# Three-round graph network on one core: the first layer's matrix applied to the features before the sum over adj

## What is computed

```python
# out = relu(adj @ x @ kernel + bias)
x = _layernorm(x + gcn(x, adj))
u = x
for _ in range(3):
    v = mlp(adj @ u, uv_W1, uv_b1, uv_W2, uv_b2, uv_W3, uv_b3)
    u = mlp(adj @ v, vu_W1, vu_b1, vu_W2, vu_b2, vu_W3, vu_b3)
return _layernorm(x + v)
```

## Time and profile before

| | |
|---|---|
| median of 3 runs | 1174.88 us (1174.84 to 1175.34) |
| the profiled execution, its time | 1174.89 us |
| its span, first to last instruction | 1173.1 us, mean granted TensorE clock 0.999 |
| TensorE, matmuls | busy 1153.4 us (98%), 5220 records |
| VectorE | busy 738.6 us (63%) |
| ScalarE | busy 665.0 us (57%) |
| DMA | 260.7 MB on the main queue, 63.8% of 16 engines |

### The profile page before, as it was taken

One profiled execution on the slowest core, in us unless ns is written; L12 is line 12 of the kernel. 1 busy time (PEld: TensorE's weight loads), 2 busy tenths in 40 slices (PEclk: granted clock), 3 DMA queues, 4 the chain that ended last, 5 costly groups with the idle time before them and its releaser, 6 DMA issues.

```text
span 1173.1 us, 13671 instructions
## 1 busy us (share of the span) xinstructions
PE 1153.4 (98%) x5220; PEld 950.3 (81%) x5220; DVE 738.6 (63%) x885; ACT 665.0 (57%) x815; POOL 0.2 (0%) x4
## 2 busy tenths in 40 slices
PE   7999999999999999999999999999999999999997
PEld 6778888888888888888888888888888888887775
DVE  7997776358555555655545746554566555668885
ACT  7765554346554555555444754554556454567885
POOL 0000000000000000000000000000000000000000
PEclk9999999999999999999999999999999999999999
DMA  9998775567366646555656736655665565569891
GB/s 367 408 365 273 242 282 199 180 215 285 110 215 215 195 164 208 205 194 184 205 188 216 256 105 226 208 169 186 203 227 185 192 205 208 196 233 354 291 325 37
DMA packets 73361, 261.61 MB, mean 223 GB/s; under 512 B 8144, under 2 KB 8784, under 8 KB 73296
## 3 DMA queue, kind: packets, MB, share of 16 engines
q1 hardware_dynamic: 73296, 260.74, 63.8%
HBM read 258.61 MB, written 2.10 MB: 222 GB/s over the span
## 4 chain that ended last, share of the span: by engine, by line
PE 90%; DMA 5%; DVE 3%; ACT 2%; issue 0%; SPq 0%; ACTq 0%
PE agg_ps L790 27%; PE agg_ps L783 27%; PE agg_ps L776 27%; DMA adj_raw<-in_adj 5%; PE pre_ps L719 4%; DVE adj_lo L673 2%; PE hid_ps L681 1%; PE hid_ps L683 1%; PE hid_ps L682 1%; ACT adj_hi L561 1%; PE hid_ps L731 1%; ACT resid L483 0%; DVE stats L571 0%; PE hid_ps L745 0%; DVE resid L586 0%
## 5 line engine op out<-in xcount | busy, mean ns | idle before, releaser
L673 DVE TENSOR_TENSOR adj_lo<-adj_raw,adj_hi 128x1024 fp32r<-128x1024 f32 x488 | 578.1, 1221 | 240.6 <-ACT adj_hi L561 233.6
L776 PE MATMUL agg_ps<-adj_hi,feat_hi 128*128 128x512 f32 x1536 | 608.9, 396 | 8.1 <-ACT adj_hi L561 8.1
L783 PE MATMUL agg_ps<-adj_hi,feat_lo 128*128 128x512 f32 x1536 | 599.1, 390 | 0.0
L561 ACT ACTIVATE adj_hi<-adj_raw 128x1024 fp32r<-128x1024 f32 x488 | 494.1, 1052 | 93.3 <-PE agg_ps L790 76.9
L790 PE MATMUL agg_ps<-adj_lo,feat_hi 128*128 128x512 f32 x1536 | 474.8, 390 | 1.8 <-DVE adj_lo L673 1.8
L776 PEld LDWEIGHTS agg_ps<-adj_hi,feat_hi 128*128 128x128 f32 x1536 | 288.9, 188 | 70.3 <-issue 11.7
L790 PEld LDWEIGHTS agg_ps<-adj_lo,feat_hi 128*128 128x128 f32 x1536 | 288.0, 188 | 64.4 <-DVE adj_lo L673 4.3
L783 PEld LDWEIGHTS agg_ps<-adj_hi,feat_lo 128*128 128x128 f32 x1536 | 289.0, 188 | 62.2 <-issue 3.4
L462 ACT ACTIVATE hid<-hid_ps,params 128x512 f32<-128x512 f32 (+1 forms) x80 | 54.5, 681 | 55.5 <-PE hid_ps L683 50.3
L527 ACT ACTIVATE in_hi<-part 128x512 fp32r<-128x512 f32 x24 | 15.2, 634 | 110.7 <-DVE part L662 110.7
L462 ACT ACTIVATE post<-pre 128x512 f32<-128x512 f32 x39 | 24.6, 630 | 79.6 <-DVE pre L642 79.6
(11 more groups left out here) (56 smaller groups left out, 262.4 us busy)
## 6 DMA issues: line engine op xcount, KB each, us to landing
adj_raw<-in_adj SPq DMA_DIRECT2D x488, 512.0 KB, 5.7
resid<-in_x SPq DMA_DIRECT2D x8, 256.0 KB, 8.8
out<-resid SPq DMA_DIRECT2D x7, 256.0 KB, 6.6
params<-in_weights SPq DMA_DIRECT2D x1, 386.0 KB, 8.1
out<-resid SPq DMA_DIRECT2D x2, 128.0 KB, 1.7
b_row<-in_bias_rows SPq DMA_DIRECT2D x1, 128.0 KB, 8.7
params<-in_weights SPq DMA_DIRECT2D x1, 64.0 KB, 7.2
b_row<-in_bias_rows SPq DMA_DIRECT2D x1, 64.0 KB, 8.8
```

Source lines behind the costliest of these rows:

```text
L561: act.activation(adj_hi[:, plan.slot[b], i * CHUNK:(i + pieces) * CHUNK], adj_raw[:, h % RAW, 0:pieces * CHUNK], ACT.Copy).then_inc(adj_hi ...
L673: dve.tensor_tensor(adj_lo[:, plan.slot[b], slot], adj_raw[:, h % RAW, 0:pieces * CHUNK], adj_hi[:, plan.slot[b], slot].bitcast(F32), ALU. ...
L776: pe.matmul(group_bank(g), feat_hi[feats][:, tile(src, i)], adj_hi[:, plan.slot[b], piece(i)], start=start, stop=False)
L783: pe.matmul(group_bank(g), feat_lo[feats][:, tile(src, i)], adj_hi[:, plan.slot[b], piece(i)], start=False, stop=False)
```

## The change

For hidden units the third layer is made like the second (`product` with hid2_hi and hid2_lo, new tiles, into pre_ps), so nodes lie on the columns, and the bias is a column that the activation of `act_post` adds. Then `pe_fold`, new, multiplies post by the first matrix of the next pass's network (four fp32 matmuls of 128 columns, which turn the tile), into the same bank pre_ps; `act_feat` copies it, rounded, to feat_hi and `dve_feat` subtracts. So the features of passes 2 to 5 are already multiplied by W1, and there `act_in`, `dve_in` and `pe_hid1` are gone: `act_hid1` works on the sum itself. Pass 1, whose features come from the layernorm, keeps the first layer (kinds IN_1 and TURN_1). The last pass loses it as well. `dve_pre` is left for the gcn and the last pass. The weights to split are five and no longer four. The table of steps is new (the kind TURN before and now, and TURN_1, are shown), the spill of a begun part to SBUF stands no earlier than act_hid1 of the unit that reads the same place, and TensorE's pe_out waits for the feat_lo of the unit before.

```diff
-    TURN: dict(dve_sum=0, act_in=0, dve_in=0, pe_hid1=4, act_hid1=5, dve_hid=4, pe_hid2=9, act_hid2=11,
-               pe_out=12, dve_pre=12, act_post=15, dve_feat=17),
...
+    TURN_1: dict(dve_sum=1, act_in=2, dve_in=2, pe_hid1=5, act_hid1=6, dve_hid=5, pe_hid2=8, act_hid2=9,
+                 dve_hid2=10, pe_out=13, act_post=14, pe_fold=16, act_feat=17, dve_feat=18),
...
+    TURN: dict(dve_sum=0, act_hid1=1, dve_hid=0, pe_hid2=4, act_hid2=5, dve_hid2=6, pe_out=9, act_post=10,
+               pe_fold=12, act_feat=13, dve_feat=14),
...
-            after_last = {"dve_pre": ends.get("dve_stats", -1), "act_std": ends.get("dve_shift", -1),
+            after_last = {"act_hid1": ends.get("pe_hid2", -1), "pe_out": ends.get("dve_feat", -1), "dve_pre": ends.get("dve_stats", -1), "act_std": ends.get("dve_shift", -1),
                           "dve_stats": ends.get("dve_norm", -1),
                           "act_post": max(ends.get("act_norm", -1) if self.steps_of(u) != END else -1,
-                                          ends.get("act_post", -1))} if tiles[0] == 0 else {}
+                                          ends.get("act_post", -1), ends.get("pe_fold", -1))} if tiles[0] == 0 else {}
...
-        return TURN if r in (0, self.rows - 1) else IN_PARTS
+        turn = r in (0, self.rows - 1)
+        if s == 1:
+            return TURN_1 if turn or r < 3 else IN_1
+        return TURN if turn else IN_PARTS
...
-    HID_W = {UV: (0, 1), VU: (2, 3), LAST: (0, 1)}
-    OUT_W = {GCN: 0, UV: 5, VU: 6, LAST: 5}
-    OUT_BIAS = {GCN: 0, UV: 1, VU: 2, LAST: 1}
+    N_WEIGHTS, N_SPLIT, N_COLS, N_ROWS = 7, 5, 6, 2
+    FIRST_W, HID_W, OUT_W = 0, {UV: 1, VU: 3, LAST: 1}, {UV: 2, VU: 4, LAST: 2}
+    GCN_RAW, FOLD_RAW = 0, {UV: 6, VU: 1}
+    COLS = {UV: (0, 1, 2), VU: (3, 4, 5), LAST: (0, 1)}
+    ROW = {GCN: 0, LAST: 1}
...
+                u = at(t, "act_feat", HIDDEN)
+                if u is not None:
+                    act.wait_ge(fold_done, deep(u) + 1)
+                    act.activation(feat_block(feat_hi, u), pre_ps[:, :], ACT.Copy).then_inc(feat_hi_ready, 1)
...
                 u = at(t, "act_post", HIDDEN)
                 if u is not None:
-                    act.wait_ge(pre_ready, u + 1)
-                    act.wait_ge(feat_lo_ready, u)
-                    prelu(post[:, :], pre[:, :]).then_inc(post_ready, 1)
-                    prelu(feat_block(feat_hi, u), pre[:, :]).then_inc(feat_hi_ready, 1)
+                    b = COLS[kind_of(u)][2]
+                    act.wait_ge(pre_done, u + 1)
+                    if deep(u):
+                        act.wait_ge(fold_done, deep(u))
+                    else:
+                        act.wait_ge(feat_lo_ready, u)
...
+                    if kind_of(u) in HIDDEN:
+                        prelu(hid2_hi[:, :], hid2_ps[:, :], bias=b_col[:, b:b + 1]).then_inc(hid2_hi_ready, 1)
+                    prelu(hid2[:, own(u)], layer_bank(0, u), bias=b_col[:, b:b + 1]).then_inc(hid2_ready, 1)
                 u = at(t, "act_hid1", DEEP)
                 if u is not None:
-                    b = HID_W[kind_of(u)][0]
-                    act.wait_ge(hid1_done, deep(u) + 1)
+                    b = COLS[kind_of(u)][0]
+                    if plan.whole(u):
+                        act.wait_ge(hid1_done, deep(u) + 1)
+                        of = hid1_ps[:, :]
+                    elif plan.summed(u):
+                        act.wait_ge(sum_kept, plan.sums(u))
+                        of = agg(u)
+                    else:
+                        act.wait_ge(half_used, agg_done(u))
+                        of = agg(u)
                     if deep(u):
                         act.wait_ge(hid2_done, deep(plan.first_of(u)))
-                    if plan.in_parts(u):
-                        prelu(hid_hi[:, :], hid1_ps[:, :], bias=b_col[:, b:b + 1]).then_inc(hid_hi_ready, 1)
-                    prelu(hid1[:, own(u)], layer_bank(0, u), bias=b_col[:, b:b + 1]).then_inc(hid1_ready, 1)
-                u = at(t, "act_in", DEEP)
-                if u is not None and plan.in_parts(u):
+                    if kind_of(u) in HIDDEN:
...
                 u = at(t, "dve_feat", HIDDEN)
                 if u is not None:
                     dve.wait_ge(feat_hi_ready, u + 1)
-                    dve.wait_ge(post_ready, deep(u) + 1)
-                    dve.tensor_tensor(feat_block(feat_lo, u), post[:, :], feat_block(feat_hi, u).bitcast(F32),
+                    dve.tensor_tensor(feat_block(feat_lo, u), pre_ps[:, :], feat_block(feat_hi, u).bitcast(F32),
...
+                u = at(t, "dve_pre", (GCN, LAST))
+                if u is not None:
...
+                u = at(t, "dve_hid2", HIDDEN)
+                if u is not None:
+                    dve.wait_ge(hid2_hi_ready, deep(u) + 1)
+                    dve.wait_ge(hid2_ready, u + 1)
+                    dve.tensor_tensor(hid2_lo[:, :], hid2[:, :], hid2_hi[:, :].bitcast(F32), ALU.subtract)\
+                       .then_inc(hid2_lo_ready, 1)
...
+                u = at(t, "pe_fold", HIDDEN)
+                if u is not None:
+                    pe.wait_ge(post_ready, deep(u) + 1)
+                    for j in tiles_of(u):
+                        last = pe.matmul(pre_ps[:, j * P:(j + 1) * P], post[:, j * P:(j + 1) * P],
+                                         w_raw[:, FOLD_RAW[kind_of(u)], :], start=True, stop=True)
+                    last.then_inc(fold_done, 1)
                 u = at(t, "pe_out", (GCN,) + DEEP)
                 if u is not None:
                     if u == 0:
                         pe.wait_ge(gcn_loaded, 32)
                     pe.wait_ge(hid2_ready, u + 1)
-                    if u:
-                        pe.wait_ge(pre_ready, plan.first_of(u))
-                    for k, j in enumerate(tiles_of(u)):
-                        last = pe.matmul(layer_bank(2, u)[:, k * P:(k + 1) * P], hid2[:, j * P:(j + 1) * P],
-                                         w_raw[:, OUT_W[kind_of(u)], :], start=True, stop=True)
+                    ahead = plan.first_of(u) - 1
+                    if ahead >= 0 and kind_of(ahead) in HIDDEN:
+                        pe.wait_ge(feat_lo_ready, ahead + 1)
+                    elif ahead >= 0:
+                        pe.wait_ge(pre_ready, norms(ahead) + 1)
+                    if kind_of(u) in HIDDEN:
+                        w = OUT_W[kind_of(u)]
+                        pe.wait_ge(hid2_lo_ready, deep(u) + 1)
+                        last = product(pre_ps[:, :], (w_hi[:, w, :], w_lo[:, w, :]), (hid2_hi[:, :], hid2_lo[:, :]))
+                    else:
+                        matrix = w_raw[:, GCN_RAW, :] if kind_of(u) == GCN else w_split[:, OUT_W[LAST], :]
+                        for k, j in enumerate(tiles_of(u)):
+                            last = pe.matmul(layer_bank(1, u)[:, k * P:(k + 1) * P], hid2[:, j * P:(j + 1) * P],
+                                             matrix, start=True, stop=True)
                     last.then_inc(pre_done, 1)
                 u = at(t, "pe_hid2", DEEP)
                 if u is not None:
...
                     last.then_inc(hid2_done, 1)
-                u = at(t, "pe_hid1", DEEP)
-                if u is not None:
-                    w = HID_W[kind_of(u)][0]
+                u = at(t, "pe_hid1", HIDDEN)
+                if u is not None:
                     if deep(u) == 0:
                         pe.wait_ge(w_lo_ready, 1)
-                    if deep(u):
-                        pe.wait_ge(hid1_ready, deep(plan.first_of(u)))
-                    if plan.in_parts(u):
-                        pe.wait_ge(in_lo_ready, plan.count_in_parts(u))
-                        last = product(hid1_ps[:, :], (w_hi[:, w, :], w_lo[:, w, :]), (in_hi[:, :], in_lo[:, :]))
-                    elif plan.summed(u):
-                        pe.wait_ge(sum_kept, plan.sums(u))
-                        last = pe.matmul(layer_bank(0, u), w_hid[:, w, :], agg(u), start=True, stop=True)
                     else:
-                        pe.wait_ge(agg_kept, plan.kept(u))
-                        last = pe.matmul(layer_bank(0, u), w_hid[:, w, :], hid1[:, own(u)], start=True, stop=True)
+                        pe.wait_ge(hid1_ready, deep(u))
+                    pe.wait_ge(in_lo_ready, plan.wholes(u))
+                    last = product(hid1_ps[:, :], (w_hi[:, FIRST_W, :], w_lo[:, FIRST_W, :]), (in_hi[:, :], in_lo[:, :]))
                     last.then_inc(hid1_done, 1)
```

121 lines of the change are left out of this document (65 added, 56 removed).

## The result

The changed kernel took 1177.12 us (median of 20 runs, 1176.30 to 1178.28), the kernel before beside it 1174.87 us (20 runs, 1174.13 to 1176.00): ratio 1.0019, 95% interval 1.0013 to 1.0024. The forecast was 1174.5 us, no change; the range (1171.4 to 1177.8) holds the result. It is 2.25 us slower: small, but resolved by these 20 runs. That the range holds the time is partly luck: the result lies 0.7 us under its upper end.

A forecast was written before the change was run, and what follows sets the result against it. The prediction took TensorE's one long stream of matmuls as the bound. Stream -0.5, entry to pass 1 +1.1, last pass -0.3 and tail -0.7 made -0.4 us, from 1174.9 to 1174.5 us; range 1171.4 to 1177.8.

The forecast's parts named there:

- the work in the stream, -0.5 us: TensorE's matmul stream: first layers gone -16.6 and -6.0, cheaper output layers -6.4, added fold +28.5; sum -0.5 us.
- The fold's 0.89: Four fp32 matmuls of 128 columns per hidden unit on TensorE, 0.89 us each time, +28.5 us over 32 units.
- The product's 0.69: One split product on TensorE, three fp32r matmuls of 512 columns, costs 0.69 us.
- no waits in the middle passes: Passes 2 to 4: the chains fit before TensorE's next step, by 0.4 us at a turn; nothing waits.
- entry to pass 1: Units 8 and 15: longer wait for in_lo, +0.5, and two waits of 0.3; together +1.1 us.
- Its first term: Entry to pass 1: a seventh adj_lo ahead of in_lo, 1.14 us, product one tick (0.68) later; +0.5 us of wait.
- the tail: Behind the stream: the normalisation's chain starts a tick earlier, -0.7 us; bounds 0 and -1.1.
- Last pass. Together -0.3 us.: Last pass's waits: -0.7 at unit 42 and others, +0.4 at unit 46; together -0.3 us.
- The bounds of -0.9 to +1.5: Last pass: all these waits go, -0.9, or the sum of unit 42 stays 2.4 us late, +1.5.
- the term of +0.4 for unit 46: Last pass, unit 46: pe_out comes 1.5 us after pe_hid2, its chain needs 1.85 us; +0.4 us.
- VectorE becomes the bound of the last pass: Slower rival, last pass: VectorE's work outlasts TensorE's, the 6.0 us saved return as waits; 1180.8 us, half 1177.8; chance 0.11.
- Neither faster nor slower by 0.2%: Whole kernel: time between 1172.5 and 1177.2 us, no change that a measurement can tell; chance 0.71.

The follow-up runs named there:

- split fold: Changed kernel with each fold issued as twelve fp32r matmuls of 128 columns on post in two parts, instead of four plain fp32 matmuls; 1203.44 us.
- mended order: Changed kernel with three step times of the last pass later and units 8 and 15 reordered at the entry to pass 1; 1174.46 us.
- the run with one number changed: Changed kernel with only the normalisation of unit 44 moved from 21 to 24 ticks, behind the last cast of adj; 1176.04 us.

## Why the prediction was wrong

**Right: the work in the stream, -0.5 us.** The fold's 0.89 was confirmed by doubling it (0.893). The product's 0.69 shows in pass 1, which has gained a fold and kept its first layer: over the five units from the 1225th adj matmul (after 2.9 us behind) to the 1897th (6.6 behind) it is 3.7 us, 0.7 each with unit 15's wait of 0.2 in it. That the middle passes come out at 0.00 proves neither price: there a unit loses one product, and swaps its four fp32 tiles for a product and gets them back as the fold, so any two prices cancel. (Pass 1 says nothing of the fold's price either, for there too fold and output layer cancel.) In the end the stream's change is 8 products more in pass 1 (5.5 us) against 7 plain layers fewer in the last (6.0). By an estimate of 0.39 us a product, from the 131 ns that the Trainium skill gives (TensorE: Matmul & The Clock Gate, Back-to-back issue gap), pass 1 would have cost 3.1 us and its waits. It cost 5.5 and its waits, so the trace disagrees with the page here too.

**Right: no waits in the middle passes**, at 4 or at 8 ticks, and the doubled fold shows room for 0.9 us of TensorE's time more in every unit. At the turns there is none for a further pass over post on the other engines: that made the three waits of the split fold.

**Right: entry to pass 1**, +1.1 forecast, 6.72 - 5.5 = +1.2 measured. It was read from one row, the seventh adj_lo ahead of in_lo; undoing it gave 1.7 us by the medians. Its first term came out at 0.67 (1.44 less 0.77) and not 0.5, since a tick is 0.68 us only on average: the products with adj_lo stand together at the end of every second tick, as the orders of the last pass in the section on the change show. The tick that the product moved holds two adj matmuls, 0.46 us, and 1.14 - 0.46 = 0.68.

**Right: the tail**, -0.7 forecast, -0.85 measured; the first activation stands 1.1 us behind the start of the last adj matmul and no longer 2.0, since the normalisation ahead of it comes earlier. That it holds the activation back, as the earlier trace rows said, shows when it moves to VectorE: by 0.3 us in after, by 1.2 in the mended order.

**Wrong: "Last pass. Together -0.3 us."** Measured: +2.0 (-3.97 against the 7 layers' -6.0). The bounds of -0.9 to +1.5 were for the other units, and there it came to -0.5 near the -0.7 taken: unit 42 gained 0.95 where I took 0.5, and unit 45 lost 0.6, by its late sum, where I took a gain of some tenths. **The step that failed is the term of +0.4 for unit 46: it was +2.5** (its stretch lost 1.7 us, where its layer's 0.86 should have been gained), and I had given it no bounds. Three parts of it can be told by the run with one number changed:
- 1.3 us: the normalisation of unit 44. I took the sum of unit 46 to be at its tick and laid its chain behind it. But its sum waits for the last casts of adj, and those stand on ScalarE in one order with the other units' steps. This had no term.
- 0.9 us where +0.4 was taken: the output layer. Between pe_hid2 and pe_out stand two adj matmuls (0.46 us) and not three (0.68), and from the start of the second layer to the output layer it took 2.27 us and not 1.85, with a std of the layernorm on ScalarE ahead of the activation (1157.12).
- 0.3 us: ahead of the second layer, not traced further.

The diff showed act_norm of LAST going from 24 to 21 ticks; I did not ask what this 1.64 us instruction now stands in front of. An instruction of its kind is in the trace before, 1.65 us, so the price was there to be read.

**The slower rival that came nearest in number, half of "VectorE becomes the bound of the last pass" (1177.8 us), is not what happened.** VectorE was busier still, 56.5 of 60 us against 53.4, though the same microseconds are some 6 us earlier in the work here:

```profile
1085.00:1145.00 60.00, 59.75 (x272) 48.19 (x271) 56.49 (x90) 50.79 (x69) 0.00 (x0) 1.00 0.94 327
...
1148.00:1160.00 12.00, 9.85 (x48) 7.29 (x47) 7.85 (x17) 8.01 (x17) 0.00 (x0) 1.00 0.06 22
```

At 94% it delayed TensorE by some tenths only: at unit 44, and at unit 45 behind this stretch, TensorE waited 0.24 us for an activation whose sum had come late from VectorE. The 0.6 us of unit 45 is what this mechanism brought over before. Where TensorE lost its time, in the second stretch, VectorE was busy for 7.9 of 12 us. The run that moved only ScalarE's normalisation of unit 44 left VectorE's work whole and took 1.3 us away.

**The chances.** "Neither faster nor slower by 0.2%" had 0.71, and 0.19% is at its very edge. None of the rivals held an order on ScalarE: the case that happened, waits at one unit of the last pass because another unit's step stands ahead of the last casts, had no chance of its own.

## What to carry to other kernels

Where a table of due times sets the order of four engines, cost every number of it that the diff changes, also of steps that are on no critical path: each moves an instruction past others on its own engine, and whoever waits behind it pays up to its duration (here 1.3 us for one of 1.64). A chain with one step fewer gains only if what feeds it (here the last casts of adj) is not pushed back by the same edit. And before old and new arithmetic are compared, the waits of both should be mended: here mending the tables was worth 1.6 us in the old kernel and 4.4 in the new one, and the arithmetic less than 1.

## Not expected of the hardware

- Plain fp32 and fp32r matmuls of 128 columns cost the same from start to start, 0.112 and 0.107 us a record, while at 512 columns a plain fp32 matmul costs 0.86 us where one of fp32r costs 0.227. So here the product in tiles of 128 columns was better left in plain fp32 (2 records a tile) than split in three.
- A wait of TensorE can cost more than its length. In the traces the granted clock fell, behind waits of 1.9 and 2.2 us, from 1.00 to 0.50, which cost 1.8 us at each turn of the split fold and 0.6 to 0.9 us in the tail; behind 1.05 and 1.30 us in the tail it stayed at 1.00 to TensorE's last matmul.
- An engine near its limit need not hold much up: VectorE was busy for 94% of 60 us and made TensorE wait for some tenths, and one misplaced instruction of 1.64 us on ScalarE, which was busy for two thirds of the time around, cost 1.3 us.
